# Attention scores from fp32r high and low parts: two heads in 96 rows, smaller and earlier loads, a sixth bias buffer

## The reference

```python
# layer 0, per batch b with expert e = itok[b]
h = gelu(x @ Wi[e] + bi[e]); r = h @ Wo0[e] + bo0[e] + x
x = layernorm(r) * gamma[e] + beta[e]
# layer 1
scale, shift = split(silu(sin_emb(t)) @ W_ada + b_ada)
x = layernorm(x) * (1 + scale) + shift
q, k, v = (x @ Wq + bq), (x @ Wk + bk), (x @ Wv + bv)      # 16 heads of 16
scores = (q / 4) @ k.T + attention_bias[b, h]               # 512 x 512 per head
probs = softmax(where(mask, -inf, scores))
x = x + (probs @ v) @ Wo + bo
x = x + gelu2((layernorm(x) * g2 + beta2) @ W1 + b1) @ W2 + b2
```

## Time and profile before

| | us |
|---|---|
| median of 3 runs (1060.62 to 1068.48) | 1063.66 |
| the profiled execution | 1060.56 |
| its span in the trace | 1058.7 |
| first stage, to the first score | 0 to 260 |
| transition, tile 0 to tile 16 | 261.4 to 306.6 |
| attention, tile 16 to the last | 306.6 to 821.3 |
| rest | 821.3 to 1058.7 |

### The profile page before, as it was taken

One profiled execution on the slowest core, in us unless ns is written; L12 is line 12 of the kernel. 1 busy time (PEld: TensorE's weight loads), 2 busy tenths in 40 slices (PEclk: granted clock), 3 DMA queues, 4 the chain that ended last, 5 costly groups with the idle time before them and its releaser, 6 DMA issues.

```text
span 1058.7 us, 19427 instructions
## 1 busy us (share of the span) xinstructions
PE 1006.1 (95%) x6870; PEld 758.3 (72%) x6936; DVE 840.7 (79%) x1966; ACT 790.2 (75%) x1291; POOL 634.2 (60%) x333
## 2 busy tenths in 40 slices
PE   5999999999799999999999999999999799999998
PEld 4789988888565655656666665666666589999997
DVE  6599999998868988989889898998988555555553
ACT  6755577555599899999999999999999344444443
POOL 3565766664246877798787997878877332222110
PEclk9999999999899999999999999999999999999999
DMA  8746788759799999998999989999895131111001
GB/s 234 263 146 222 247 295 301 276 180 378 304 330 398 409 373 358 352 340 322 367 355 340 357 322 362 345 347 343 313 338 199 40 120 60 60 61 40 21 20 40
DMA packets 103249, 269.44 MB, mean 254 GB/s; under 512 B 7522, under 2 KB 63586, under 8 KB 86642
## 3 DMA queue, kind: packets, MB, share of 16 engines
q1 hardware_dynamic: 103154, 268.21, 70.5%
HBM read 217.57 MB, written 50.61 MB: 253 GB/s over the span
## 4 chain that ended last, share of the span: by engine, by line
PE 49%; DVE 12%; DMA 12%; POOL 10%; ACT 8%; issue 7%; SPq 2%; DVEq 0%; ACTq 0%; POOLq 0%
PE psH L540 11%; DMA t_bt<-in_fside_Bx16xSxS 10%; PE psO L540 10%; PE psT L650 9%; POOL t_bt L1423 8%; PE psQ L540 5%; PE psV L663 5%; PE psS L639 4%; ACT t_bt L894 3%; DVE t_x L1026 2%; SPq L255 2%; PE psA L540 2%; ACT t_pt L780 2%; DVE t_bt L1215 2%; PE psX L692 1%
## 5 line engine op out<-in xcount | busy, mean ns | idle before, releaser
L1423 POOL TENSOR_TENSOR t_bt<-t_bt,t_mb 128x1024 f32<-128x1024 f32 x182 | 384.6, 2147 | 89.0 <-DMA t_bt<-in_fside_Bx16xSxS 88.8
L1215 DVE CUSTOM_DVE_ANT_0 t_bt<-psS,t_bt 128x512 f32<-128x512 f32 x512 | 338.2, 684 | 61.1 <-PE psS L639 39.6
L894 ACT ACTIVATE t_bt<-t_bt,t_nm 128x512 f32<-128x512 f32 x512 | 356.6, 732 | 20.4 <-DVE t_nm L1215 20.3
L650 PE MATMUL psT<-t_idf,t_bt 128*128 128x128 f32 x2048 | 308.6, 274 | 5.2 <-issue 2.5
L650 PEld LDWEIGHTS psT<-t_idf,t_bt 128*128 128x128 f32 x2048 | 252.9, 141 | 66.0 <-ACT t_bt L894 12.7
L780 ACT ACTIVATE t_pt<-psT 128x512 f32<-128x512 f32 x317 | 191.2, 603 | 18.9 <-PE psT L650 18.2
L639 PE MATMUL psS<-t_ks,t_qs 128*128 128x512 bf16 x482 | 183.9, 382 | 8.0 <-DVE t_nm L1215 3.7
L1225 DVE COPY t_pt<-psT 128x512 f32<-128x512 f32 x195 | 133.8, 686 | 1.7 <-PE psT L650 1.7
L663 PE MATMUL psV<-t_pt,t_vs 128*17 128x512 f32 x1024 | 134.2, 598 | 0.0
L639 PEld LDWEIGHTS psS<-t_ks,t_qs 128*128 128x128 bf16 x512 | 50.0, 98 | 83.0 <-DVE t_nm L1215 62.8
L1357 POOL TENSOR_SCALAR t_crs<-t_cmv 128x4 f32<-128x4 f32 x8 | 4.2, 519 | 134.8 <-DVE t_cmv L1018 134.8
(11 more groups left out here) (171 smaller groups left out, 2045.1 us busy)
## 6 DMA issues: line engine op xcount, KB each, us to landing
t_bt<-in_fside_Bx16xSxS SPq DMA_DIRECT2D x128, 1024.0 KB, 7.4
sc_qk<-t_parts SPq DMA_DIRECT2D x32, 768.0 KB, 6.6
t_qs<-sc_qk SPq DMA_DIRECT2D x16, 1024.0 KB, 9.8
t_ks<-sc_qk SPq DMA_DIRECT2D x16, 1024.0 KB, 12.2
t_wo_f<-in_L_cond_Wo SPq DMA_DIRECT2D x8, 1024.0 KB, 7.5
sc_qk<-t_parts SPq DMA_DIRECT2D x16, 512.0 KB, 7.4
t_wi_f<-in_L_cond_Wi SPq DMA_DIRECT2D x7, 1024.0 KB, 5.3
sc_v<-t_v SPq DMA_DIRECT2D x8, 544.0 KB, 7.6
```

Source lines behind the costliest of these rows:

```text
L650: ins = e.transpose(psT[turned_bank(n)][:, kk, :], bt[u % NB][:, t, kk * 128:(kk + 1) * 128], idf[:, :])
L894: e.activation(p, p, ACT.Exp, bias=nm[:, n % 16:n % 16 + 1], scale=-1.0).then_inc(a_exp, 1)
L1215: e.tensor_tensor_reduce(bt[u % NB][:, t, :], s, bt[u % NB][:, t, :], -1.0, 3.0e38, ALU.add, ALU.min, nm[:, n % 16:n % 16 + 1]).then_inc(v ...
L1423: e.tensor_tensor(bt[u % NB][:, hs, :], bt[u % NB][:, hs, :], mb[b % 2][:, hs, :], ALU.add).then_inc(g_M, 1)
```

## The change

- q and k are split in two fp32r parts, high and low. ACT writes the high part straight from PSUM with the bias (the scale 1/4 now sits in Wq and bq); DVE makes the low part straight from PSUM with one scalar_tensor_tensor (psum + bias - high). `qf`, `qr`, `rest`, `low` and `third` are gone. Both instructions are per 128x512 half, four of each per batch.
- Three products (high-high, high-low, low-high) in 3 x 16 = 48 rows. The k rows of two heads stand together in 96 rows; the q of each head has its own 96 rows, zero in the other head's 48. So a score matmul is fp32r with 96 rows in place of bf16 with 128.
- POOL zeroes the two q buffers once (two memsets of 128x2048 fp32, after its first stage and `p_hid` 64); `load_qk` waits for it (`g_z`).
- DRAM holds 3 fp32 blocks instead of 8 bf16 ones. Loads are per quarter batch (4 heads): two of 192 KB for q, one of 384 KB for k, issued at tile 16m + 4 for tile 16(m + 1); the first is issued where the first was, the second before the transition. `load_v(0)` moves behind `load_qk(1)`.
- `NB` is 6.
- k of a batch (of all but the last two) goes to psH instead of psQ; `hidden` of the next batch waits for DVE's low part of it, and v waits for DVE's low part of q where it waited for ACT.

```diff
-TERMS = [(0, 0), (0, 1), (0, 2), (1, 0), (1, 1), (1, 2), (2, 0), (2, 1)]
-NP3 = len(TERMS)
-KR = HD * NP3
+KR = 3 * HD
-NB, NP, NS, EARLY, MORE = 5, 8, 3, 5, 21
+NB, NP, NS, EARLY, MORE = 6, 8, 3, 5, 21
...
-            qs, ks = [sbuf(st, "qs0", [KR, 8, S], BF16)], [sbuf(st, "ks0", [KR, 8, S], BF16)]
+            qs, ks = [sbuf(st, "qs0", [128, 2, 2, S])], [sbuf(st, "ks0", [128, 2, S])]
...
+        def qk_bank(b, n, mt):
+
+            return psH[mt] if n and b < B - 2 else psQ[mt]
...
             def store_part(b, n, a):
-                P.wait_ge(g_p2, 2 * b + n + 1)
+                P.wait_ge(v_ql, 4 * b + 2 * n + 2)
...
             def load_qk(n):
-                b, half = divmod(n, 2)
-                P.wait_ge(p_sc, 32 * (n - 1))
+                b, part = divmod(n, 4)
+                P.wait_ge(g_z, n % 2 + 1)
+                P.wait_ge(p_sc, 16 * (n - 1))
...
-                for dst, w in ((qs, 0), (ks, 1)):
-                    load(d_q[n % 2], dst[n % 2][:, :, :], sc_qk[b, w, :, :, half, :].rearrange("(h d) i s -> (d i) h s", d=HD))
+                js = slice(part % 2 * 2, part % 2 * 2 + 2)
+                for g in range(2):
+                    src = sc_qk[b, 0, :, :, part // 2, :].rearrange("(j g d) i s -> g (d i) j s", g=2, d=HD)
+                    load(d_q[n % 2], qs[n % 2][KR * g:KR * g + KR, :, g, :], src[g][:, js, :])
+                src = sc_qk[b, 1, :, :, part // 2, :].rearrange("(j g d) i s -> (g d i) j s", g=2, d=HD)
+                load(d_q[n % 2], ks[n % 2][0:2 * KR, :, :], src[:, js, :])
...
+                if m < NK and b > 2:
+                    P.wait_ge(v_ql, 4 * (b - 3) + NK + m + 1)
...
-                    P.wait_ge(a_qf, 4 * b + 3 + half)
+                    P.wait_ge(v_ql, 4 * b + half + 1 + (0 if b < B - 2 else NK))
...
-                e.matmul(s, qs[g % 2][:, h % 8, t * 128:(t + 1) * 128], ks[g % 2][:, h % 8, :], start=on_pool(u), stop=True).then_inc(p_sc, 1)
+                e.matmul(s, qs[g % 2][0:2 * KR, u % 4 // 2, u % 2, t * 128:(t + 1) * 128].bitcast(F32R), ks[g % 2][0:2 * KR, u % 4 // 2, :].bitcast(F32R),
+                         start=on_pool(u), stop=True).then_inc(p_sc, 1)
...
-            def rest(b, n):
-                P.wait_ge(a_p0, 2 * b + n + 1)
-                P.wait_ge(g_p2, 2 * (b - 1) + n + 1)
-                P.wait_ge(d_ssb, 16)
-                e.tensor_tensor(qr[n][:, :, :], qf[n][:, :, :], parts[n][:, 0, :, :], ALU.subtract).then_inc(v_qr, 1)
-
             def qkv(b):
                 for n in range(2):
-                    yield
-                    yield
-                    rest(b, n)
+                    for mt in range(NK):
+                        yield
+                        P.wait_ge(a_qh, 4 * b + 2 * n + mt + 1)
+                        e.scalar_tensor_tensor(out=parts[n][:, 1, mt, :].bitcast(F32R), in0=qk_bank(b, n, mt)[:, :], scalar=bqk[:, n, mt:mt + 1], in1=parts[n][:, 0, mt, :],
+                                               op0=ALU.add, op1=ALU.subtract).then_inc(v_ql, 1)
...
             first_stage()
+            P.wait_ge(p_hid, NM * B)
+            for q in qs:
+                e.memset(q[:, :, :, :], 0.0).then_inc(g_z, 1)
```

More of the change, by code:

```diff
@@ L336, in store_part @@
             def store_part(b, n, a):
-                P.wait_ge(g_p2, 2 * b + n + 1)
+                P.wait_ge(v_ql, 4 * b + 2 * n + 2)
                 dst = sc_qk[b, n].rearrange("p i k s -> p i (k s)")
                 src = parts[n][:, :, :, :].rearrange("p c k s -> p c (k s)")
-                g = slice(3 * a, min(3 * a + 3, NP3))
-                k = g.stop - g.start
-                load(d_p[n], dst[:, g, :], src[:, 0:k, :] if n else src[:, a:a + 1, :].broadcast_to([128, k, NK * S]))
+                if n == 0 and a == 0:
+                    load(d_p[n], dst[:, 0:2, :], src[:, 0:1, :].broadcast_to([128, 2, NK * S]))
+                elif n == 0:
+                    load(d_p[n], dst[:, 2:3, :], src[:, 1:2, :])
+                elif a == 0:
+                    load(d_p[n], dst[:, 0:2, :], src[:, 0:2, :])
+                else:
+                    load(d_p[n], dst[:, 2:3, :], src[:, 0:1, :])
             def store_parts(b, n):
-                for a in range(3):
+                for a in range(2):
                     store_part(b, n, a)
@@ L476, in sync_program @@
                 load_bias(u)
+            load_qk(1)
+            load_v(0)
             nextb, at = NB, 0
@@ L583, in qkv @@
                         P.wait_ge(v_x2Tl, NK * (b + 1))
[L584 to L586 removed]
+                        if n and b < B - 2:
+                            P.wait_ge(v_hTl, 8 * (b + 2) + NH + mt + 1)
+                        elif n:
+                            P.wait_ge(v_ql, 4 * b + mt + 1)
+                        mm3(qk_bank(b, n, mt)[:, :], [([u[:, kk, ms] for u in wsm[w]], [z[:, kk, :] for z in x2T]) for kk in range(NK)], p_q)
                         yield
@@ L807, in split_small @@
                 P.wait_ge(d_w, 128)
-                for n in "qkv":
-                    copy(wsm[n][0][:, :, :], wstage[n][:, 0:NK, :], a_wsm)
+                for n, scale in zip("qkv", (0.25, 1.0, 1.0)):
+                    e.activation(wsm[n][0][:, :, :], wstage[n][:, 0:NK, :], ACT.Copy, scale=scale).then_inc(a_wsm, 1)
             def hidden(b, m):
@@ L825, in turn_x2 @@
                     copy(x2T[0][:, kk, :], psQ[kk][:, :], a_x2Th)
-            def low(b, n):
-                P.wait_ge(v_qr, 2 * b + n + 1)
-                P.wait_ge(g_p2, 2 * b + n - 1)
-                copy(parts[n][:, 1, :, :], qr[n][:, :, :], a_p1)
             def qkv(b):
-                for n, scale in enumerate((0.25, 1.0)):
+                for n in range(2):
                     for mt in range(NK):
@@ L836, in qkv @@
                         P.wait_ge(v_bq, 1)
-                        P.wait_ge(v_qr, 2 * (b - 1) + n + 1)
                         P.wait_ge(d_ssb, 16)
-                        e.activation(qf[n][:, mt, :], psQ[mt][:, :], ACT.Identity, bias=bqk[:, n, mt:mt + 1], scale=scale).then_inc(a_qf, 1)
+                        P.wait_ge(d_p[n], PT * b)
+                        e.activation(parts[n][:, 0, mt, :].bitcast(F32R), qk_bank(b, n, mt)[:, :], ACT.Identity, bias=bqk[:, n, mt:mt + 1]).then_inc(a_qh, 1)
                         yield
-                    P.wait_ge(a_qf, 4 * b + 2 * n + 2)
-                    P.wait_ge(d_p[n], PT * b)
-                    copy(parts[n][:, 0, :, :], qf[n][:, :, :], a_p0)
-                    if n:
-                        low(b, 0)
                 for half in range(2):
-                    if half == 0:
-                        low(b, 1)
                     yield
@@ L1088, in split_small @@
                 e.tensor_scalar(bqk[:, 0, :], bqk[:, 0, :], 0.25, None, ALU.mult).then_inc(v_bq, 1)
-                for i, n in enumerate("qkv"):
+                for i, (n, scale) in enumerate(zip("qkv", (0.25, 1.0, 1.0))):
                     P.wait_ge(a_wsm, i + 1)
-                    low(wsm[n][1][:, :, :], wstage[n][:, 0:NK, :], wsm[n][0][:, :, :], v_wsm)
+                    e.scalar_tensor_tensor(out=wsm[n][1][:, :, :], in0=wstage[n][:, 0:NK, :], scalar=scale, in1=wsm[n][0][:, :, :].bitcast(F32),
+                                           op0=ALU.mult, op1=ALU.subtract).then_inc(v_wsm, 1)
             def hidden(b, m):
@@ L1390, in split_wi @@
                 low(wi_s[1][:, :, :], wi_f[:, :, :], wi_s[0][:, :, :], g_wil)
-            def third(b):
-                for n in range(2):
-                    P.wait_ge(a_p1, 2 * b + n + 1)
-                    P.wait_ge(d_p[n], PT * b)
-                    e.tensor_tensor(parts[n][:, 2, :, :], qr[n][:, :, :], parts[n][:, 1, :, :], ALU.subtract).then_inc(g_p2, 1)
             def first_stage():
@@ L1468, in gpsimd_program @@
             root(rs[1], mv[1], 1e-5, (v_var2, B), g_rs2)
-            for b in (B - 2, B - 1):
-                if b == B - 2:
-                    while at < 4:
-                        attention(at)
-                        at += 1
-                else:
-                    while at < 14:
-                        attention(at)
-                        at += 1
-                third(b)
             while at <= N + LAG - 1:
```

58 lines of the change are left out of this document (26 added, 32 removed).

## The result

The changed kernel takes 1070.89 us in the median of 14 runs (1064.95 to 1078.08), against 1061.05 us (1057.8 to 1068.48, 14 runs) for the kernel before on the same chip: ratio 1.008, 95% interval 1.0049 to 1.011. It is slower by 0.8%. That is clear of the spread, though inside the 1% that the prediction had set as no change. The forecast of 1041 us was wrong in sign, and the result lies outside its range.

What follows compares the result with a forecast made beforehand. PE was taken as nearly full, with ACT and DVE close in attention. First stage -3.5, start +1, transition -7 and attention -12 gave -21.5 on 1060.56, 1039; between two bases it said 1041 us, range 1027 to 1058.

Steps and rivals of the forecast that it cites:

- First stage: First stage: DVE is early for h, a turn falls from 32.45 to PE's own 31.8 us; -3.5 us (0 to -4).
- start: Start of attention: the first q and k load waits for POOL's memset, taken as 2 us; +1 us (0 to +4).
- transition: Between first stage and attention: DVE's stretched norms and waits go, PE's clock partly recovers; -7 us (-2 to -10).
- The lateness goes nearly all: Attention: earlier bias loads and smaller q and k loads remove DVE's 17.4 us of waits; groups 16.64 to 16.25, -12 us.
- PE's sum: Attention: PE's own work per group of 16 tiles, 15.6 us before and 15.9 after the change.
- The prediction's last sign: Attention: the forecast is wrong if groups stay above 16.6 us with bias waits gone; coupling was then the price.
- second rival: Attention: the longer weight load shows where PE's queue is dry; +23 us for half the tiles, +46 for all; 6%.
- 118-ns argument: Attention: weight load of 190 ns hides under 256-column matmuls 118 ns apart in the first stage, so it costs 0.
- third rival: Attention: q and k land late, PE waits at each 16th tile; landing at 13.5 us gives 1078 us; 6%.
- The sixth buffer: Attention: the sixth bias buffer lets loads go 16 tiles ahead instead of 12 and itself costs no engine anything.
- the first: Rival: PE becomes the bound, every 17 ns ends up in the time, most gain kept; 1053 us, 20%.
- the fifth: Rival: bias waits stay because DMA engines are busy for 0.93 of attention; attention +2, 1056 us; 6%.

Runs made afterwards that it cites:

- e3: The kernel before with quarter-batch loads of q and k, issued 12 tiles ahead, and six bias buffers: 1059.31 us, ratio 0.9981.
- e2: The changed kernel with bf16 scores in the first half of each fp32 row, same loads, third parts left out: 1058.79 us, ratio 0.9987.
- x1: The changed kernel with the same bytes of q and k loaded into all 128 rows, scores of other numbers: 1059.26 us, ratio 0.9984.
- x2: The changed kernel with the same 48, 48 and 96 rows, each in one 4 KB piece, scores of other numbers: 1069.16 us, ratio 1.0083.
- f3: The changed kernel with q and k as bf16 high and low parts, half the bytes, third parts left out: 1047.99 us, ratio 0.9865.
- g1: The changed kernel timed once more, nothing altered: 1069.0 us, ratio 1.0076.
- g2: The changed kernel with DVE's small once-a-batch result t_na written with a stride of two: 1069.4 us, ratio 1.0069.
- e1: The changed kernel with five bias buffers instead of six: 1066.21 us, ratio 1.0045.
- g3: f3 with five bias buffers instead of six: 1045.55 us, ratio 0.9845.
- g4: The kernel before with only the quarter-batch loads of q and k, five bias buffers: 1057.78 us, ratio 0.9953.

## Why the prediction was wrong

**First stage, start and transition were right.** The turn fell to 31.69 (31.8 forecast), a memset took 1.8 us (two in 3.55, POOL's row above; 2 forecast), tile 0 began at 256.9 (257 to 258), 4.5 us earlier where the terms gave 2.5, and tiles 0 to 16 lost 7.8 us (7). Low parts of 0.75 us against the 0.69 taken are within the bounds.

**The step that failed is the attention's: "The lateness goes nearly all", and -12 from it.** It has four errors, and the ledger's +16.2 for tiles 16 to 511 stands 28 us above the forecast.

1. *PE's sum was too small, and so coupling and lateness too large.* I made it 15.6 a group before and 15.9 after. From the chains above it is 16 x (0.215 + 0.44) + 4 x 0.215 for the masks + 4 x (0.98 + 0.10) + 0.44 = 16.1 before, and 16.1 + 13 x 0.02 + 3 x 0.11 = 16.7 after. From tile 128 on a group took 16.47 in the mean before (394.3 / 383 x 16) and 16.93 after. So in this stretch some 0.4 us a group was not PE's, and e3 shows that next to none of it was lateness; what lateness cost was 3.4 us at tiles 16 to 128. Of the 17.4 us that were read as bias waits of DVE 7.4 were waits for PE, "remote" being a missing record and not a landing, and the other 10.0 overlapped PE's own time for the most part. The prediction's last sign has come true: groups above 16.6 with the bias waits gone.

2. *PE's extra was twice as much, and about a third of it was absorbed, not all.* The forecast took 17 ns x 495 = 8.5 us as paid for by the lateness, and the weight load as free. The extra is 0.6 us a group, some 14 us for tiles 128 to 511, and e2 says that 8.8 of them show there. The second rival named the weight load, but priced it for half or all of the tiles (23 or 46 us); it opens only behind three of four products with v, some 93 in 495 tiles, 0.11 us more each than before, 10 us in all. The 118-ns argument was right for weight loads between full matmuls, and wrong for those behind a product of 17 columns. The factor of two between the loads, which the prediction took from its rows and set beside the Trainium skill (TensorE: Matmul & The Clock Gate, on weight-path modes), held: 98 and 190 ns.

3. *Half the bytes were weighed, the rows were not.* The forecast counted q and k as 0.79 MB per 16 tiles and took the rate as given. Loads into 48 and 96 rows made the DMA engines slower: x1 against the changed kernel, 6.6 us in the profile of tiles 16 to 511 (530.9 to 524.3), and 10 us in the medians of x1 and x2. Against its third rival the prediction set the landing of q; k, which comes behind it, landed after 12.2 us in the median before and after 8.9 now. As the engines were full in tiles 16 to 128, this shows there as late k, most of it by PE's waits above; DVE waits for no mask there. This is the third rival's mechanism by another price: not each 16th tile, but one to three of them, while a queue stands.

4. *The sixth buffer*, which was said to cost no engine anything, cost 2 to 4 us in three pairs of runs, in f3 by way of POOL and DVE.

The ledger for tiles 16 to 511 doesn't close wholly. e3, the kernel before with the lateness gone, takes 510.6 us and the changed kernel 530.9. Of these 20.3 us, bf16 scores take back 8.3 (e2: 522.6) and full rows 6.6 (x1: 524.3). If the two add, some 5 us are left, of which no run shows the parts; `t_na` is a candidate, with 10.8 us in all for e3's 5.1. Of the rivals, the first ("every 17 ns ends up in the time") had the right engine, with a gain left over that did not exist; the fifth ("half a megabyte less doesn't change" the DMA engines' share) had the right suspect, and its price too low.

What stays open: why x1 gains 10 us in the medians and 7.8 in the profiled executions. The slower runs of the changed kernel lose more in the crowded stretch (tiles 16 to 128 take 125.7 us at a span of 1063.2, 128.3 in g1 at 1066.2, 130.0 in g2 at 1070.6), which fits; e1, with 130.0 at 1065.2, has five buffers. No trace of a run of 1078 was taken.

The version that beats both is g3, 1045.55 us: first stage and layout as changed, bf16 pairs and five buffers, at the price of the third parts. With all parts kept, the fastest is g4, 1057.78 us. The full-row load for fp32r parts was tried only with scores of other numbers; it alone would be near the kernel before.

## What to carry to other kernels

Before booking the removal of a wait, add up the next engine to its last open row (here the score behind a product with v, 0.11 us more each): a wait that overlaps another engine's full time is worth only what that engine has left. A releaser that the profile can't name is not a landing until something shows it; look for a record that is missing. A transfer is priced by rows as well as bytes: the same bytes into 48 or 96 rows instead of 128 cost 10 us of 1061, most of it where the DMA engines are full. More buffers let an engine run without pauses, and a small instruction elsewhere may be living off those pauses.

## What the hardware did that I had not expected

- Loads of equal bytes: 334 GB/s at a DMA share of 0.97 with 48 and 96 rows (in pieces of 2 KB or 4 KB), 348 at 0.94 with 128 rows; in the later stretch 310 at 0.93 and 311 at 0.87.
- A DVE instruction of 0.16 us (tensor_scalar, 128x4, fp32) took 5.77 us beside three masks of POOL in a row, the first of them already running; with a stride in its output it still took up to 1.92; the custom scores instruction beside it (PSUM and SBUF input) keeps its 0.68 us.
- The weight load of a 128-column score lies open behind a product with 17 stationary columns: 0.10 us for bf16, 0.20 us for fp32r. Behind the transposes, where the fp32r score costs 0.235, no such part shows.
